# Turning the FFNs' normalised rows by a transposing transfer of two fp16 halves instead of on TensorE

## What is computed

```
x = x + 0.5 * ffn(layernorm(x))
x = x + attention(layernorm(x))
x = x + 0.5 * ffn(layernorm(x))          # the same weights again

ffn(y), 16 experts, C = 256, H = 128:
  logits = l2norm(y) @ l2norm(sim) - sigmoid(gates)
  w      = softmax over the chosen experts (positive logits, or the top 2)
  q,k,v  = sum over e of w[n,e] * (y[n] @ proj[e])       # 256 -> 128 each
  ao     = causal softmax(q k' / sqrt(128)) v            # within a sequence of 512
  out    = sum over e of w[n,e] * (ao[n] @ o_proj[e])    # 128 -> 256
```

## Time and profile before

| | us |
|---|---|
| median of 3 runs | 2592.98 (2592.41 to 2593.59) |
| the profiled execution | 2595.07 |
| its span, first to last instruction | 2593.2 |
| the profiled execution beyond its span | 1.87 |
| PE busy | 2499.9 (96%) |
| PE's weight loads busy | 2285.9 (88%) |
| DVE busy | 2153.8 (83%) |
| ACT busy / POOL busy | 944.7 (36%) / 954.5 (37%) |
| mean granted TensorE clock | 0.988 of 2.4 GHz |

### The profile page before, as it was taken

How to read it: one execution, slowest core, us unless ns; L and a number is a source line. 1 busy time by engine, 2 the same in 40 slices (tenths; PEclk the granted TensorE clock), 3 DMA queues, 4 the chain that set the end, 5 groups by cost and what they waited for, 6 DMA issues and landing times. The chain is left out here.

```text
span 2593.2 us, 45059 instructions
## 1 busy us (share of the span) xinstructions
PE 2499.9 (96%) x13966; PEld 2285.9 (88%) x13966; DVE 2153.8 (83%) x6164; ACT 944.7 (36%) x2546; POOL 954.5 (37%) x2010
## 2 busy tenths in 40 slices
PE   6999999999997999999999999997999999999998
PEld 6999999999995888888888888886899999999997
DVE  6888888888886888888888888886888888888887
ACT  3111101101103777777777777774111101101100
POOL 4333333333334434343434444344333333333331
PEclk9999999999998999999999999998999999999999
DMA  6000000000012544454554545455100000000000
GB/s 190 11 8 9 6 8 9 6 8 9 10 36 62 92 88 90 89 93 92 87 90 90 92 92 89 86 98 129 39 9 18 12 9 18 13 9 18 15 6 22
DMA packets 419056, 127.08 MB, mean 49 GB/s; under 512 B 378880, under 2 KB 417792, under 8 KB 418816
## 3 DMA queue, kind: packets, MB, share of 16 engines
q1 hardware_dynamic: 418816, 124.20, 24.1%
HBM read 26.24 MB, written 4.19 MB: 12 GB/s over the span
## 5 line engine op out<-in xcount | busy, mean ns | idle before, releaser
L583 PE MATMUL ffn_ring<-ffn_mix_weights,ffn_yT 128*128 128x384 f32 x5760 | 1133.2, 341 | 6.7 <-DVE ffn_mix_weights L828 4.0
L583 PEld LDWEIGHTS ffn_ring<-ffn_mix_weights,ffn_yT 128*128 128x128 f32 x5760 | 1008.6, 189 | 53.1 <-DVE ffn_mix_sums L757 17.9
L759 DVE SCALAR_TENSOR_TENSOR ffn_mix_sums<-ffn_ring,ffn_w,ffn_mix_sums 128x384 f32<-128x384 f32 x896 | 551.7, 616 | 229.1 <-PE ffn_ring L583 207.0
L637 PE MATMUL ffn_ring<-ffn_out_weights,ffn_avT 128*128 128x512 f32 x1536 | 443.3, 399 | 7.5 <-POOL ffn_avT L1085 5.7
L1605 ACT ACTIVATE attn_exponentials<-attn_exponentials,attn_score_neg_max 128x512 f32<-128x512 f32 (+3 forms) x512 | 285.8, 559 | 164.3 <-DVE attn_score_neg_max L1520 163.7
L1673 POOL CAST attn_probsT_long<-attn_turned_long 128x1024 fp32r<-128x1024 f16 (+1 forms) x256 | 233.1, 939 | 253.6 <-DVE attn_probs L1537 253.1
L637 PEld LDWEIGHTS ffn_ring<-ffn_out_weights,ffn_avT 128*128 128x128 f32 x1536 | 283.0, 189 | 37.9 <-POOL ffn_avT L1085 7.4
L1537 DVE SCALAR_TENSOR_TENSOR attn_probs<-attn_exponentials,attn_prob_factor,attn_probs 128x512 f16<-128x512 f32 (+3 forms) x512 | 248.2, 546 | 17.3 <-ACT attn_probs L1614 17.0
L1614 ACT ACTIVATE attn_probs<-attn_exponentials,attn_prob_factor 128x512 f16<-128x512 f32 (+3 forms) x512 | 250.2, 552 | 25.0 <-DVE attn_prob_factor L1530 15.8
L924 ACT ACTIVATE ffn_yT<-ffn_transposes 128x256 fp32r<-128x256 f32 x64 | 24.6, 384 | 639.6 <-PE ffn_transposes L553 639.6
L774 DVE SCALAR_TENSOR_TENSOR x<-ffn_ring,ffn_w_out,x 128x256 f32<-128x256 f32 x512 | 246.5, 481 | 13.0 <-PE ffn_ring L637 7.3
(11 more groups left out here) (152 smaller groups left out, 3145.0 us busy)
## 6 DMA issues: line engine op xcount, KB each, us to landing
ffn_mix_stage<-in_L_ffn_q_proj_dram SPq DMA_DIRECT2D x32, 128.0 KB, 2.6
ffn_mix_stage<-in_L_ffn_k_proj_dram SPq DMA_DIRECT2D x32, 128.0 KB, 2.6
ffn_mix_stage<-in_L_ffn_v_proj_dram SPq DMA_DIRECT2D x32, 128.0 KB, 2.9
ffn_out_stage<-in_L_ffn_o_proj_dram SPq DMA_DIRECT2D x16, 256.0 KB, 2.9
out_dram<-x SPq DMA_DIRECT2D x8, 512.0 KB, 3.1
x<-in_L_attn_x_dram SPq DMA_DIRECT2D x7, 512.0 KB, 8.8
early_stage<-in_L_attn_w_q_dram SPq DMA_DIRECT2D x4, 512.0 KB, 5.1
attn_dense_stage<-in_L_attn_w_dense_dram SPq DMA_DIRECT2D x4, 512.0 KB, 4.5
```

Source lines behind the costliest of these rows:

```text
L583: last = pe.matmul(bank[:, 0:QKV], yT[:, t % 2, h, k * P:(k + 1) * P], mix_half(e, wh)[:, k], start=(n == 0), stop=(n == 3 * CK - 1))
L637: last = pe.matmul(bank[:], avT[:, t % 2, h], wo[:, g, wh], start=(i == 0), stop=(i == 2))
L759: dve.scalar_tensor_tensor(into, bank[:, 0:QKV], w[:, t, e:e + 1], into, ALU.mult, ALU.add).then_inc(mix_done, 1)
```

## The change

For tiles 4 to 31 of both FFNs, 56 tiles in all, y no longer passes PE. ACT writes y times 2^11 as fp16 (`y16_high`, at e = 5 of slot T-2, ahead of its squares), DVE writes the rest of y times 2^11 as a second fp16 half (`y16_low`, at e = 6, ahead of `score_max`), SP turns the 128 x 512 halves in one transposing transfer (`turn_y`, ahead of `turn_probs` in its queue), and POOL multiplies what has landed by 2^-11 into `yT`, both halves in one instruction (`cast_y`, at the very start of slot T-1, ahead of `merge_qkv`). PE's `transpose_y`, ACT's `split_y` and DVE's `split_y` stay for tiles 0 to 3 only. `y_turned` shares its memory with the scratch output of ACT's squares, hence the new wait there; two scratch tensors of the constants share that of `y16`.

```diff
+Y_SCALE = 2.0 ** 11
+Y_ON_PE = 4
...
+        y_turned = nc.alloc_sbuf_tensor_at(f"{name}_y_turned", [P, 2 * C], F16, offset=nc.sbuf_base)
+        y_sq = sb("y_squares", [P, C])
+        y16_at = nc.sbuf_base
+        y16 = sb("y_halves", [P, CK, 2, P], F16)
...
+            def turn_y(T):
+
+                sp.wait_ge(yT_tr, T + 1)
+                sp.wait_ge(yT_lo, T)
+                sp.wait_ge(ss_done, T + 1)
+                sp.dma_start_transpose(y_turned[:].rearrange("p (j q) -> p j q", q=P),
+                                       y16[:].rearrange("p k h c -> p (k h c)")).then_inc(y_landed, 16)
...
+                if Y_ON_PE <= T + 3 < TILES:
+                    turn_y(T + 3)
                 turn_probs(T)
...  # PE: mix_first
-                pe.wait_ge(yT_hi, T + 1)
+                if T < Y_ON_PE:
+                    pe.wait_ge(yT_hi, T + 1)
                 pe.wait_ge(yT_lo, T + 1)
...  # PE: transpose_qk
-                pe.wait_ge(yT_lo, (T + 3) if inside(T + 2, 0) else TILES)
+                if T + 2 < Y_ON_PE:
+                    pe.wait_ge(yT_lo, T + 3)
...  # PE: slot
-                    if e == 0 and inside(T, -1):
+                    if e == 0 and T + 1 < Y_ON_PE:
                         transpose_y(T + 1, (t + 1) % QT)
...  # DVE
+            def y16_low(T, t):
+                dve.wait_ge(yT_hi, T + 1)
+                dve.scalar_tensor_tensor(y16[:, :, 1], y[:, t % 2].rearrange("p (k c) -> p k c", c=P), Y_SCALE, y16[:, :, 0],
+                                         ALU.mult, ALU.subtract).then_inc(yT_tr, 1)
...
-                    if e == 0 and inside(T, -1):
+                    if e == 0 and T + 1 < Y_ON_PE:
                         split_y(T + 1, nxt)
...
+                        if e == 6 and Y_ON_PE <= T + 2 < TILES:
+                            y16_low(T + 2, nn)
...  # ACT: y_squares
+                if T > Y_ON_PE:
+                    act.wait_ge(yT_lo, T)
...
+            def y16_high(T, t):
+                act.wait_ge(y_done, T + 1)
+
+                reach(act, y_landed, 16 * (T - Y_ON_PE))
+                act.activation(y16[:, :, 0], y[:, t % 2].rearrange("p (k c) -> p k c", c=P), ACT.Copy,
+                               scale=Y_SCALE).then_inc(yT_hi, 1)
...
-                    if e == 0 and inside(T, -1):
+                    if e == 0 and T + 1 < Y_ON_PE:
                         split_y(T + 1, (t + 1) % QT)
+                    if e == 5 and Y_ON_PE <= T + 2 < TILES:
+                        y16_high(T + 2, (t + 2) % QT)
...  # POOL
+            def cast_y(T, t):
+                pool.wait_ge(y_landed, 16 * (T - Y_ON_PE + 1))
+
+                pool.wait_ge(mix_ready, (E - 1) * (T - 1))
+                pool.tensor_scalar(yT[:, t % 2].rearrange("p h (k q) -> p k h q", q=P),
+                                   y_turned[:].rearrange("p (k h q) -> p k h q", h=2, q=P), 1.0 / Y_SCALE, None,
+                                   ALU.mult).then_inc(yT_lo, 1)
...
+                if Y_ON_PE <= T + 1 < TILES:
+                    cast_y(T + 1, nxt)
                 if inside(T, 1):
                     merge_qkv(T - 1, prev)
```

More of the change, by code:

```diff
@@ L154, with __init__ @@
 class Constants:
-    def __init__(self, nc, ctx, m):
+    def __init__(self, nc, ctx, m, at):
         def sb(n, shape):
@@ L164, in __init__ @@
         self.sim = sb("sim", [P, CK, E])
-        self.sq = sb("sim_sq", [P, CK, E])
+        self.sq = nc.alloc_sbuf_tensor_at("sim_sq", [P, CK, E], F32, offset=at)
         self.norm = sb("sim_norm", [P, E])
         self.rnorm = sb("sim_rnorm", [P, E])
-        self.simn = sb("sim_unit", [P, CK, E])
+        self.simn = nc.alloc_sbuf_tensor_at("sim_unit", [P, CK, E], F32, offset=at + 4 * CK * E)
         self.gate = sb("gate_rows", [P, E])
@@ L320, in ffn @@
         y = sb("y", [P, 2, C])
-        y_sq = sb("y_squares", [P, C])
         y_ss = sb("y_sum_squares", [P, 2])
@@ L365, in ffn @@
         pt = ps("probs_av")
-        const = Constants(nc, ctx, m) if aw else None
+        const = Constants(nc, ctx, m, y16_at) if aw else None
         if aw:
@@ L386, in ffn @@
         pt_free, pt_hi, pt_lo, av_ready = sem("prob_free"), sem("pt_hi"), sem("pt_lo"), sem("av_rdy")
-        t_landed = sem("prob_landed")
+        t_landed, y_landed = sem("prob_landed"), sem("y_landed")
         av_half_done, av_done, av_hi, av_lo = sem("av_half"), sem("av"), sem("av_hi"), sem("av_lo")
```

## The result

The changed kernel takes 2622.97 us (median of 5 runs, 2622.14 to 2624.91) against 2592.98 us before (median of 5, 2589.81 to 2594.14): a ratio of 1.0127, 95% interval 1.0117 to 1.0138. It is 30 us slower, where no change was forecast with 0.64 and the range ended at 2603.5.

A forecast was written before the change was run, and what follows sets the result against it. PE is full, but the slot loop of PE's e = 2 to e = 14 and DVE's list bounds it, hiding the transposes' 12.3 us. All engine terms sum to 0: 2593.0 us, own range 2591 to 2595, stretched to 2603.5.

The forecast's parts named there:

- PE, 0: PE at e = 2: 0.22 us less transpose work a tile, 0.22 us more waiting; 0 x 56 = 0.
- the wait at e = 2: PE's e = 2 load waiting for DVE's sum of expert 0: 17.9 us in all, to grow to about 30.
- the two loads: PE's load of the output product at e = 15 and the waiting e = 2 load: to stay 2.81 us apart.
- reading of slot 31: Slot 31 has no transposes, yet the same 2.81 us between loads; idle time grew from 0.26 to 0.47 us.
- DVE's list: DVE's work from e = 14 to the sum of expert 0, 2.76 us, said to cover PE's transposes.
- DVE, ACT and SP, 0: DVE's moved split, ACT's swapped copy and SP's extra transfer a tile: each claimed to cost 0.
- Rival 3: Probabilities come late through y16_low and the second transfer: 25 us slower, 2618 us; chance 0.05.
- POOL, 0: cast_y before mix_first, taken as 0.7 us, nearest to the copy, ends 0.3 us inside the 1.01 available: 0.
- the rate of two-input operations: Upper end for cast_y's length on POOL: 0.275 us for each 128 more columns, giving 1.29 us.
- Rival 1: POOL's cast_y at the two-input rate ends 0.28 us late for mix_first: 9.5 us slower, 2602.5 us; chance 0.19.
- the 0.11 us of lateness: Part of a late mix_first load to cost little or nothing, from e = 2: 0.26 us idle, matmuls 1.16 against 1.05.
- The deciding length of 1.01 us: POOL's time from cast_y's start to mix_first's load, less 0.05 us; a longer cast brings rival 1.

The follow-up runs named there:

- experiment 4: Kernel before, DVE's copy of half the attention result given to ACT: 2590.65 us, ratio 1.000; also without transposes of tiles 4 to 31: 2590.38 us.
- experiment 5: PE's e = 2 wait moved from expert 0's sum to the last output sum: kernel before 2584.01 us; changed kernel, cast ahead of merge_x, 2569.39 us.
- cast_before_merge: Changed kernel with POOL's cast moved ahead of merge_x, at the end of the slot before: 2603.93 us, ratio 1.005 to the kernel before.
- order_fold_bank_wait: Changed kernel, cast ahead of merge_x as plain copy, factor in gate weights, e = 2 wait on last output sum: 2569.76 us, 0.9925 of before.
- after_order_av_on_act: Changed kernel, cast ahead of merge_x, DVE's copy of half the attention result given to ACT: 2590.12 us, ratio 1.0002 to the kernel before.

## Why the prediction was wrong

- **PE, 0.** Right: the wait at e = 2 went to 30.0 us, the two loads stayed 2.82 us apart, and leaving the transposes out of the old kernel gave 1.000. The reading of slot 31 was a sound trial.
- **Its reason** was right in kind and short in detail. "DVE's list" from e = 14 was called the cover, and 12.3 us were promised if it were over 0.2 us shorter. Made 0.38 us shorter it gave nothing (experiment 4), since DVE then waits for PE's last output product, which lies ahead of the transposes as well. What gives it is the wait itself (experiment 5).
- **DVE, ACT and SP, 0.** Right: with the copy in the multiply's place the whole change costs 0.05%, with an interval that takes in 0. Rival 3 did not happen.
- **POOL, 0.** This is the step that failed, at "I take 0.7 us, nearest to the copy". It measured 1.504, so the cast ended late where 0.3 us were to be left. The bounds were wrong as well: the rate of two-input operations was taken as the worst, and a multiply of one input runs at 2.5 ns a column, slower than their 2.15 (0.275 for 128). The proof of "one input runs at the copy's rate" was another operation, the affine select, and the only row shown of the same operation, the 0.273 us for 16 columns, was used for its start alone. The same view has more of this operation, which could have given a rate:

```profile
L1046 POOL TENSOR_SCALAR ffn_gate_active<-ffn_gate_logits 128x16 f32<-128x16 f32 x25 | 6.3, 253 | 0.0
L1012 POOL TENSOR_SCALAR ffn_ln_var_eps<-ffn_ln_mean_var 128x1 f32<-128x1 f32 x25 | 5.8, 232 | 16.8 <-DVE ffn_ln_mean_var L682 16.8
```

  From one column to sixteen it is 21 ns here and 41 with L1038, so 1.4 to 2.7 ns a column, and an estimate for 512 of 0.95 to 1.6 us. That is too rough to fix the length, but most of it lies over 1.01. The Trainium skill's 769 ns, from the GPSIMD Engine Reference, section 3.1, is half of the measured time too.
- **Rival 1** was the case that came, with the mechanism and the place as told, and too small a price: 9.5 us instead of 30. Its length was 0.21 us short. The multiply starts 0.11 us later than L1062 did (0.82 behind merge_x's start instead of 0.71; the copy in its place starts 0.68 behind). And of the 0.11 us of lateness that was to cost nothing only 0.06 is free: of 0.61 us of waiting PE loses 0.55, of which 0.45 ahead of the first expert and 0.10 in the next product. The 0.11 in the earlier trace rows is what a late load cost at e = 2, and says little of what is hidden elsewhere. Why less is hidden at the first expert was not tested; the product ahead of it is one of 384 columns, ahead of e = 2 one of 512. The deciding length of 1.01 us was not tested closely: 0.611 was early, 1.504 late.

## What to carry to other kernels

When an engine that seems full waits briefly once a loop, find what that wait stands for before taking work off the engine: all work between the wait's cause and the wait is free, and taking it away buys only waiting, until the wait is moved to what the buffer really needs. A step new to an engine must be priced by a row of the very operation, and if there is none, the worst rate in the trace is no upper bound; here a scale on a copy cost 0.9 us and could be folded into a factor that was applied anyway. And moving an operation to an idle place on its engine can stretch a short one on another, if that one starts right behind it.

## What the runs showed of the hardware

- A multiply by a constant on POOL, fp16 to fp32r, 128 x 512, takes 1.504 us; with 0.859 for 256 columns that is 0.21 at its start and 2.5 ns a column. A cast of the same operands takes 0.611.
- DVE's gate weights, a 128 x 16 operation from SBUF to SBUF of 0.226 us, did not end until 0.64 us after POOL's cast had begun, whenever they fell into its first part. Started 0.17 us into it, they took 0.466 us (0.17 + 0.47 = 0.64, cast_before_merge). In order_fold_bank_wait, beside the copy of 0.61 us, they started 0.31 us in and took 0.331 (0.64 again), in one slot 0.03 us in and took 0.61. Started 0.55 us into the multiply they took 0.23 and were free (after_order_av_on_act). So the copy and the multiply, 0.61 and 1.50 us long, held DVE up for the same 0.64 us; what they hold in that time was not tried.
